# Cross-attention on one core: fewer and larger copies, earlier context loads, less clearing, and one exponential tile in four unsplit

## What is computed

```python
q = (x @ Wq).reshape(B, N, HEADS, hd).transpose(0, 2, 1, 3)
k = (context @ Wk).reshape(B, M, HEADS, hd).transpose(0, 2, 1, 3)
v = (context @ Wv).reshape(B, M, HEADS, hd).transpose(0, 2, 1, 3)
scores = jnp.einsum('bhid,bhjd->bhij', q, k) * scale
scores = jnp.where(context_mask[:, None, None, :], scores, max_neg)
attn = jax.nn.softmax(scores, axis=-1)
out = jnp.einsum('bhij,bhjd->bhid', attn, v)
```

## Time and profile before

| | |
|---|---|
| median of 3 runs | 4101.87 us |
| the profiled execution | 4104.39 us |
| its span | 4102.5 us |
| busy PE, PEld | 3330.3 us (81%), 2553.6 us (62%) |
| busy DVE, ACT, POOL | 2647.3 (65%), 2227.0 (54%), 1061.0 (26%) |
| granted TensorE clock over the span | 0.913 |
| first score product to last value product of the stage | 1752.7 to 2790.6 us |

### The profile page before, as it was taken

One profiled execution on the slowest core, in us unless ns is written; L12 is line 12 of the kernel. 1 busy time (PEld: TensorE's weight loads), 2 busy tenths in 40 slices (PEclk: granted clock), 3 DMA queues, 4 the chain that ended last, 5 costly groups with the idle time before them and its releaser, 6 DMA issues. The chain is left out here.

```text
span 4102.5 us, 50439 instructions
## 1 busy us (share of the span) xinstructions
PE 3330.3 (81%) x15064; PEld 2553.6 (62%) x15064; DVE 2647.3 (65%) x4397; ACT 2227.0 (54%) x4058; POOL 1061.0 (26%) x1139
## 2 busy tenths in 40 slices
PE   5899999999999996377877778775729989950799
PEld 4687877777787875244554455543518877740587
DVE  5787777777777774555655566565653349977554
ACT  4676767667676763155655555563122224448665
POOL 1233333232323232044544444453300000000000
PEclk9999999999999998688988898897969999985899
DMA  4444443444434432333333333324642237779775
GB/s 128 127 131 124 139 123 124 131 134 120 133 120 129 131 108 70 88 96 93 75 88 91 91 80 87 92 61 162 227 141 92 110 118 265 273 279 410 245 247 194
DMA packets 294941, 582.43 MB, mean 142 GB/s; under 512 B 37672, under 2 KB 119600, under 8 KB 280384
## 3 DMA queue, kind: packets, MB, share of 16 engines
q1 hardware_dynamic: 282048, 554.61, 42.6%
q10 hardware_dynamic: 12672, 25.17, 1.7%
HBM read 339.49 MB, written 172.79 MB: 125 GB/s over the span
## 5 line engine op out<-in xcount | busy, mean ns | idle before, releaser
L1555 DVE TENSOR_REDUCE ca_negm<-ca_mx 128x1 fp32r<-128x512 f32 x512 | 353.2, 690 | 433.2 <-PE ca_mx L1701 426.1
L640 POOL TENSOR_SCALAR sa_ex<-sa_ex,sa_rs 128x512 f32<-128x512 f32 x512 | 356.7, 697 | 952.3 <-DVE sa_rs L518 952.3
L513 DVE TENSOR_REDUCE sa_nm<-sa_st 128x1 f32<-128x512 f32 x512 | 351.1, 686 | 269.3 <-PE sa_st L747 268.2
L704 PE MATMUL sa_pj<-sa_xh,sa_w 128*128 128x512 f32 x1536 | 459.7, 419 | 11.7 <-DVE sa_kl L496 9.8
L389 ACT ACTIVATE sa_eh<-sa_tr 128x512 fp32r<-128x512 f32 x512 | 306.7, 599 | 293.9 <-PE sa_tr L757 290.8
L1628 POOL TENSOR_TENSOR ca_el<-ca_ex,ca_eh 128x512 fp32r<-128x512 f32 x256 | 365.5, 1429 | 164.8 <-ACT ca_eh L1484 163.9
L382 ACT ACTIVATE sa_ex<-sa_st,sa_nm 128x512 f32<-128x512 f32 x512 | 351.2, 686 | 58.2 <-DVE sa_nm L513 54.9
L522 DVE TENSOR_TENSOR sa_el<-sa_tr,sa_eh 128x512 fp32r<-128x512 f32 x512 | 351.2, 686 | 36.9 <-ACT sa_eh L389 30.1
L1476 ACT ACTIVATE ca_ex<-ca_st 128x512 f32<-128x512 f32 x512 | 298.2, 589 | 79.2 <-PE ca_st L1719 78.1
L1731 PE MATMUL ca_ov<-ca_eh,ca_vc 128*66 128x512 f32 x512 | 226.7, 443 | 120.0 <-ACT ca_osb L1491 72.2
L757 PE MATMUL sa_tr<-top_ident,sa_ex 128*128 128x128 f32 x2048 | 309.7, 274 | 0.2 <-POOL sa_ex L640 0.2
(11 more groups left out here) (244 smaller groups left out, 7695.9 us busy)
## 6 DMA issues: line engine op xcount, KB each, us to landing
sa_w<-w_split SPq DMA_DIRECT2D x56, 1536.0 KB, 7.4
up_g<-gate SPq DMA_DIRECT2D x50, 512.0 KB, 4.4
gate<-gate_ev SPq DMA_DIRECT2D x24, 1024.0 KB, 3.8
gate<-up_g SPq DMA_DIRECT2D x48, 512.0 KB, 2.9
up<-up_ev SPq DMA_DIRECT2D x24, 1024.0 KB, 5.6
mul_a<-gate SPq DMA_DIRECT2D x48, 512.0 KB, 12.0
mul_b<-up SPq DMA_DIRECT2D x48, 512.0 KB, 13.0
dn_a<-gate SPq DMA_DIRECT2D x96, 256.0 KB, 3.5
```

Of the source, the lines that this page charges most:

```text
L513: nc.vector.tensor_reduce(nm[:, u % U:u % U + 1], st[:, u % 2], AX_X, ALU.max, negate=True).then_inc(dve_mx, 1)
L640: nc.gpsimd.tensor_scalar(ex[:, u % U], ex[:, u % U], rs[:, u % U:u % U + 1], 1.0, ALU.mult, ALU.mult).then_inc(pool_n, 1)
L704: yield nc.tensor.matmul(pj[:, bank], w[:, n % 2, m, part, k], xx[:, b % 2, k], start=(i == 0 and k == 0), stop=(i == 2 and k == DK - 1))
L1555: nc.vector.tensor_reduce(negm[:, n % 2, qt, h:h + 1], mx[:, m % 2], AX_X, ALU.max, negate=True).then_inc(dve_mx, 1)
```

## The change

In the cross-attention stage:

1. The columns of the key and query weights are stored in another order when they are split (`columns`, `split_columns`), so that head j's column d comes to partition 4 d + j of the projections. One DMA from all 128 partitions then fills one part of all four heads (`stack`). A step's stack copies are 3 for keys and 3 for queries, all in slot 8, with one for the mask and, in slot 5, one for the maximum rows. One semaphore for each place of the ring stands for all of them.
2. `cr` has four buffers; all four context tiles of the next batch are loaded in slot 1 of a step with s % 4 = 0. The mask is loaded before x.
3. q4 and k4 are no longer cleared; POOL sets their two rows of ones, and DVE only the ones columns of vc. ACT and DVE no longer wait for this, SP and PE do.
4. Tiles with a % 8 = 3 and 7 are not split: `product` makes one plain float32 matmul of the values and `ex`. ACT then has 4 of 8 high parts, POOL 2; POOL and DVE 3 low parts each. The buffer of `ex` of such a tile is free when its product is made.

```diff
@@ cross_attention_stage
-    HIGH = ("act", "pool", "act", "dve", "act", "pool", "act", "act")
-    LOW = ("pool", "dve", "pool", "dve", "pool", "dve", "pool", "dve")
+    HIGH = ("act", "pool", "act", "", "act", "pool", "act", "")
+    LOW = ("pool", "dve", "pool", "", "pool", "dve", "dve", "")
-        cr = sp.sb("cr", [P, 2, CD])
+        cr = sp.sb("cr", [P, NT, CD])
+        def columns(tile, n):
+
+            if CK <= n < 2 * CK:
+                return tile
+            return tile.rearrange("p (g j d) -> p g d j", j=HS, d=XD)
+
+        def split_columns(tile, n):
+
+            if CK <= n < 2 * CK:
+                return tile
+            return tile.rearrange("p (g d j) -> p g d j", j=HS, d=XD)
@@ sync
+            def stack(n, tile, src, part):
+                e.dma_start(f32(tile[part * XD:(part + 1) * XD, n % RING]), f32(src[:, :])
+                            ).then_inc(stacked[n % RING], 16)
+            def stack_keys(n):
+                r = n % RING
                 if n >= RING:
                     e.wait_ge(pe_st, U * (n - RING) + U)
+                e.dma_start(f32(k4[MR:MR + 1, r]), env["mask_n"][n // XG:n // XG + 1, :].partition_broadcast(HS)).then_inc(stacked[r], 16)
+                e.wait_ge(act_kh, n + 1)
+                stack(n, k4, kh, 0)
+                stack(n, k4, kh, 1)
+                e.wait_ge(pool_kl, n + 1)
+                stack(n, k4, kl, 2)
+            def stack_queries(n):
+                e.wait_ge(act_qh, n + 1)
+                stack(n, q4, qh, 0)
+                stack(n, q4, qh, 2)
+                e.wait_ge(dve_ql, n + 1)
+                stack(n, q4, ql, 1)
             def max_rows(n):
                 e.wait_ge(act_mr, n + 1)
-                for j in range(HS):
-                    e.dma_start(f32(q4[MR + 1:MR + 2, n % RING, j]), f32(mrow[j:j + 1, :])).then_inc(mr_in[n % RING], 16)
+                e.dma_start(f32(q4[MR + 1:MR + 2, n % RING]), f32(mrow[:, :])
+                            ).then_inc(mr_in[n % RING], 16)
...
-                if t == 5 and n < N:
-                    stack_keys(n, range(3), 0)
-                    stack_keys(n, range(3), 1)
-                if t == 7 and n < N:
-                    stack_keys(n, range(3), 2)
                 if t == 8 and n < N:
-                    for part in range(3):
-                        stack_keys(n, range(3, 4), part)
-                    mask_row(n)
-                    for j in range(HS):
-                        stack_queries(n, j)
-                if t == 3 and s >= 0 and s % XG == 1 and s // XG + 1 < B:
-                    load_context(NT * (s // XG + 1))
-                    load_context(NT * (s // XG + 1) + 1)
-                if t in (8, 10) and context_tile(s, t - 1) is not None:
-                    load_context(context_tile(s, t - 1) + 1)
+                    stack_keys(n)
+                    stack_queries(n)
+                if t == 1 and s >= 0 and s % XG == 0 and s // XG + 1 < B:
+                    for i in range(NT):
+                        load_context(NT * (s // XG + 1) + i)
@@ scalar
             def exponent(a):
                 e.wait_ge(pe_st, a + 1)
-                if a >= EX:
+                if a >= EX and LOW[a % 8 - EX]:
                     wait_low(e, a - EX)
+                elif a >= EX:
+                    e.wait_ge(pe_av, a - EX + 1)
...
-                nc.scalar.activation(w_hi[:, n], w_raw[:, n % 2], ACT.Copy).then_inc(act_w, 1)
+                nc.scalar.activation(split_columns(w_hi[:, n], n), columns(w_raw[:, n % 2], n), ACT.Copy).then_inc(act_w, 1)
@@ vector
-            nc.vector.memset(f32(q4[:]), 0.0).then_inc(zeroed, 1)
-            nc.vector.memset(f32(k4[:]), 0.0).then_inc(zeroed, 1)
-            e.wait_ge(zeroed, 2)
-            nc.vector.memset(f32(q4[MR:MR + 2]), 1.0).then_inc(zeroed, 1)
-            nc.vector.memset(f32(k4[MR:MR + 2]), 1.0).then_inc(zeroed, 1)
-            nc.vector.memset(f32(vc[:]), 1.0).then_inc(zeroed, 1)
+            nc.vector.memset(f32(vc[:, :, :, :, 2 * XD:VW]), 1.0).then_inc(ones_set, 1)
@@ gpsimd
+            nc.gpsimd.memset(f32(q4[MR:MR + 2]), 1.0).then_inc(ones_set, 1)
+            nc.gpsimd.memset(f32(k4[MR:MR + 2]), 1.0).then_inc(ones_set, 1)
@@ tensor, product(a)
-                wait_low(e, a)
+                if LOW[a % 8]:
+                    wait_low(e, a)
+                else:
+                    e.wait_ge(act_ex, a + 1)
...
                 values = vc[:, b % 2, kt, HS * g + h]
+                if not LOW[a % 8]:
+                    nc.tensor.matmul(ov[0:VW, :], f32(values), ex[:, a % EX], start=(kt == 0),
+                                     stop=(kt == NT - 1)).then_inc(pe_av, 1)
+                    return
                 nc.tensor.matmul(ov[0:VW, :], values, eh[:, a % EL], start=(kt == 0), stop=False)
                 nc.tensor.matmul(ov[0:VW, :], values, el[:, a % EL], start=False, stop=(kt == NT - 1)).then_inc(pe_av, 1)
```

More of the change, by code:

```diff
@@ L42 @@
 WQMAX = 7.0
-ZEROED = 5
+ONES = 3
 BIG = float(2.0 ** 100)
@@ L1273, in cross_attention_stage @@
         dve_w = sp.sem("dve_w")
-        zeroed = sp.sem("zeroed")
-        cr_in = [sp.sem(f"cr_in{i}") for i in range(2)]
+        ones_set = sp.sem("ones_set")
+        cr_in = [sp.sem(f"cr_in{i}") for i in range(NT)]
         xq_in = sp.sem("xq_in")
@@ L1290, in cross_attention_stage @@
         dve_vl = sp.sem("dve_vl")
-        stacked = [[sp.sem(f"stacked{r}{j}") for j in range(HS)] for r in range(RING)]
-        mask_in = [sp.sem(f"mask_in{r}") for r in range(RING)]
+        stacked = [sp.sem(f"stacked{r}") for r in range(RING)]
         pe_mx = sp.sem("pe_mx")
@@ L1344, in load_context @@
             def load_context(j):
-                if j >= 2:
-                    e.wait_ge(pe_ct, j - 1)
-                e.dma_start(cr[:, j % 2], xs[j]).then_inc(cr_in[j % 2], 16)
+                if j >= NT:
+                    e.wait_ge(pe_ct, j - NT + 1)
+                e.dma_start(cr[:, j % NT], xs[j]).then_inc(cr_in[j % NT], 16)
             def load_x(b):
@@ L1358, in load_mask @@
                 e.dma_start(maskb[:, :], env["mask_f"][b:b + 1, :].partition_broadcast(P)).then_inc(maskb_in, 16)
-            def stack_keys(n, heads, part):
+            def stack(n, tile, src, part):
+                e.dma_start(f32(tile[part * XD:(part + 1) * XD, n % RING]), f32(src[:, :])
+                            ).then_inc(stacked[n % RING], 16)
+            def stack_keys(n):
                 r = n % RING
-                if part == 2:
-                    e.wait_ge(pool_kl, n + 1)
-                else:
-                    e.wait_ge(act_kh, n + 1)
-                for j in heads:
-                    if n >= RING:
-                        e.wait_ge(pe_st, U * (n - RING) + NT * j + NT)
-                    src = kl if part == 2 else kh
-                    e.dma_start(f32(k4[part * XD:(part + 1) * XD, r, j]), f32(src[j * XD:(j + 1) * XD, :])
-                                ).then_inc(stacked[r][j], 16)
@@ L1399, in outputs @@
                             ).then_inc(o_out[j % 2], 16)
-            for i in range(2):
-                load_context(i)
+            load_context(0)
             load_weights(0)
             load_weights(1)
-            for i in range(2, NT):
+            for i in range(1, NT):
                 load_context(i)
@@ L1412, in _ @@
                 load_weights(n)
-            e.wait_ge(zeroed, ZEROED)
+            e.wait_ge(ones_set, ONES)
             for G, s, t in slots():
@@ L1419, in _ @@
                     max_rows(s)
[L1420 to L1435 removed]
+                if t == 8 and n < N:
+                    stack_keys(n)
[3 more added lines that the diff above has]
+                        load_context(NT * (s // XG + 1) + i)
                 if t == 9 and s >= 0 and s % XG == 1 and s // XG + 1 < B:
+                    load_mask(s // XG + 1)
                     load_x(s // XG + 1)
[L1438 removed]
             for i in range(2):
@@ L1451, in high_key @@
                 if n:
-                    for j in range(HS):
-                        e.wait_ge(stacked[(n - 1) % RING][j], 96 * ((n - 1) // RING) + 96)
+                    e.wait_ge(stacked[(n - 1) % RING], STACKS * ((n - 1) // RING) + STACKS)
                 nc.scalar.activation(kh[:, :], km[:, :], ACT.Copy).then_inc(act_kh, 1)
@@ L1659, in transpose_context @@
                 for k in range(CK):
-                    last = nc.tensor.transpose(ms[:, cols(k)], cr[:, j % 2, cols(k)], ident[:, :])
+                    last = nc.tensor.transpose(ms[:, cols(k)], cr[:, j % NT, cols(k)], ident[:, :])
                 last.then_inc(pe_ct, 1)
```

29 lines of the change are left out of this document (8 added, 21 removed).

## The result

The changed kernel takes 3936.22 us (median of 4 runs, 3935.61 to 3937.34); the kernel before took 4103.49 beside it (4 runs, 4101.55 to 4108.8). The ratio is 0.9591, with an interval of 0.9574 to 0.9607: 167 us faster, 101 us above the 3835 forecast and 6 us beyond the upper end of the range. The direction was right, the size was not.

The account below looks back on a forecast made before the run. TensorE was taken as the nearest, not tight, bound, stalled behind SyncE's full queue; 232 us in the stage, 30 at the start and 6 in the first copies, 268 together, gave 3835 us, range 3785 to 3930.

Parts of the forecast that it names:

- The queue: Cross-attention stage, SyncE: 32 issues a step become 8, some 10 us of issuing; the seven copies land before slot 2.
- The context: Cross-attention stage: tiles loaded a step earlier into four buffers remove an 18.6 us stall per kind 1 step, 130.2 us of waits.
- rival B: Queue not relieved or copies late: steps keep near 28 us, only context and start are gained, 3938 us; chance 0.16.
- The start: Kernel start, before the first score product: less clearing and fewer first copies save 36 us, 30 and 6.
- the clearing: Kernel start: five VectorE memsets shrink to one small one, two go to GpSimd; 30 us gained.
- the first copies: First step, before the first maximum product: 19 issues (12 us) shrink to 7 (4.4 us); 6 us gained, between 0 and 8.
- The unsplit tile: Value products, one tile in four unsplit: ScalarE's slot falls to 1.05 us, PE trades two fp32r matmuls for one plain float32.
- P: Price on PE of one plain float32 matmul of 512 columns: taken as 0.94 us, wrong if outside 0.8 to 1.1.
- A: Rival on the value products: plain float32 costs 1.74 us, giving 3920 us; chance 0.10.
- C: Rival on the value products: plain float32 costs 0.44 us, ScalarE bounds, giving 3787 us; chance 0.08.
- bare slots: Slots without projections: 1.2 us forecast from 1.34; staying at 1.34 would mean order of work, not amount, sets their pace.
- Rival D: Slower: the plain product leaves TensorE at its lower clock, stage 1372 us instead of 806; chance 0.03.

Follow-up runs that it names:

- the kernel with four large copies: Changed kernel with the second copies of kh and qh left out from the fourth step on, four of six large copies kept: 3897.66 us.
- the repaired one: Changed kernel with the x load in two separately issued halves and four result buffers: 3880.09 us with unsplit tiles, 3862.15 us with all tiles split.
- x in two parts: Changed kernel with the high half of x issued in slot 7 and the low half in slot 13, each with its own semaphore: 3887.62 us.

## Why the prediction was right or wrong

**The queue: the step that failed.** The prediction had the seven copies "needed in slot 2 of the next step, ten slots or over 12 us later", found 14 us for them one after the other, and then wrote "overlapped they need far less". They do not. From the first issue at 1978.63 to the maximum product at 1993.86 it is 15.2 us, over the one-by-one 14, though the large copies are six and not seven: 1.5 MB, while the mask row has 8 KB. The 14 also priced a copy of 256 KB at the 2.0 us of one of 64 KB. The argument for overlap was the 0.63 us from issue to issue with 2.0 us to landing, at 64 KB each; with four times the bytes at the same spacing it had no row under it. The row to read was the sum of bytes over the time, and the prediction never made it. The cost of this alone is PE's wait for ca_q: about 1.5 us in each of 15 steps, kinds 1 and 2, as the kernel with four large copies shows for kind 1 (25.0 for 26.5).

The same sentence named what is queued behind the copies and went on: "only the x and mask loads and the outputs of slot 12". That *only* is the larger mistake. Nobody waits for the issue of x, but PE waits for its landing, 12.7 to 15.7 us after the issue since it moves only behind the copies, and an output that can't be issued holds ScalarE's buffer. Taking x out, or issuing it elsewhere, gives 53 and 49 us; buffers that no longer wait for the stores give 14, or some 7 once x is cured. Both together, 3936 to 3880, are 56 us of the 93 by which the steps were too long.

**The context: right in kind, wrong in what was late next.** The stall of 18.6 us and the clock after it went, and no wait for ca_cr is left. But "what is late next is TensorE itself" was wrong: the stall had been the time in which x landed. The context alone brings 88 us where 130 stood in the prediction; kind 1 fell by 22 us and kind 2 rose by 10. I took the earlier trace rows as a list of prices, each to be had by removing its wait. Had I asked of every load issued or in flight during the stall when it goes out, when it lands and who needs it, the x loads, issued at 2062.72 with 9.0 us to landing, and ScalarE's slot-by-slot waits behind the same queue, would have been on the path at once. This also means that rival B, which had "the context and the start are gained alone" at 3938, came to the right time by a wrong account. Issuing does not go by bytes (0.6 us for 256 KB), the copies do land late, the steps of kinds 0, 1 and 3 were relieved all the same, and the loss sits in the one kind that B had left untouched.

What the queue change brought is seen by subtraction only: from 4014.75 (context alone) to 3908.89 (context, queue, clearing) are 106 us, 31 of them the clearing, so some 75. In the steps of kinds 0 and 3 it is plain: 26.7 to 23.8 and 29.5 to 26.1, all tiles split.

**The start: right in the clearing, lucky in the sum.** The first projection came at 1673.95 against 1677 forecast, 33.4 us earlier; undoing the clearing costs 31 us where 30 were in the sum. The first score came 33.8 us earlier for 36 forecast, so the first copies, at 6 us in the sum, brought 0.4; the 3.4 us that the clearing brought beyond its 30 hide most of that miss. Two terms within the clearing were off and hidden. The memset on GpSimd takes 5.21 us, not the 9.5 worked out from the ratio of subtractions. And the read with a stride costs. Timelines after, GpSimd and then ScalarE with a strided and a plain split of a weight tile:

```profile
1643.98 5.21 POOL L1619 MEMSET ca_q<- 2x6144 f32 x1 [7.24 <-POOLq L67]
...
1647.18 1.09 ACT L1491 ACTIVATE ca_w_hi<-ca_w_raw 128x512 fp32r<-128x512 f32 x1 [7.80 <-DMA ca_w_raw<-in_L_xattn_Wk_dram]
1653.54 0.63 ACT L1491 ACTIVATE ca_w_hi<-ca_w_raw 128x512 fp32r<-128x512 f32 x1
```

1.09 us for 0.63, and on VectorE 1.04 for 0.69: 0.8 us for each of 7 tiles, some 6 us of engine time, within the 0 to 9 of the prediction. It does not show in the time, as the prediction took it, since loads end the waits there. The Trainium skill (SBUF — State Buffer, Door 1: The DMA port swizzle) says that a read which crosses to a new 16-byte line each time is penalised; the trace agrees that this read, with a stride of 128 bytes, costs more, and these rows are its size here.

**The unsplit tile: the price right, its worth wrong.** A plain float32 product has two records of 590 ns. Group of the value line, and a stretch of PE's timeline around one:

```profile
L1724 PE MATMUL ca_ov<-ca_ex,ca_vc x256: 590/592/1061, 1727.4 to 2621.5; 128*66 128x512 f32 x128
...
1941.75 1.02 PE L1724 MATMUL ca_ov<-ca_ex,ca_vc 128*66 128x512 f32 x2
1942.21 0.80 PE L1708 MATMUL ca_st<-ca_q,ca_k 98*128 98x512 f32 x1
1942.85 0.40 PE L1690 MATMUL ca_mx<-ca_k,ca_q 97*128 97x512 f32 x1
```

From 1941.75 to 1942.85 lie the product and one matmul of 0.234 (the score product, whose row starts before the second pass is through), so P is 0.87 us, two passes of 0.43; 0.94 was forecast, and rivals A (1.74) and C (0.44) fall. The Trainium skill had two answers: the four passes of FP8 and Floating Point Precision (TensorE Precision Notes) agree with 0.87, which is four times 0.22. The factor of four that TensorE: Matmul & The Clock Gate (Terms, the row on the xbus) gives the transpose does not hold against a real product here: 512 columns cost twice the four transposes of 0.109.

What failed is the slot. "The 0.2 above the sum shrinks to 0.15" put bare slots at 1.2 us. Counted from one maximum product to the next they average 1.30 after in kind 0, for 1.35 with all tiles split and 1.34 before: 0.05 gained of 0.14. The prediction had named an outcome close to this, bare slots that stay at 1.34: their pace comes from the order of the work and not from its amount. ScalarE, VectorE and GpSimd had less work and the slot got hardly shorter, while PE's 0.4 us a tile was paid where PE is the bound: the two slots with projections that have an unsplit product last 2.03 us for 1.63. So the unsplit tiles cost 27 us of the changed kernel and 18 of the repaired one. Kinds 0 and 3 missed by 0.7 us each. In kind 0 it is the bare slots: nine of them 0.10 too low are 0.9 us, while its seven slots with projections took (24.2 - 9 x 1.30 - 0.35)/7 = 1.74, close to the 1.76 forecast.

**The clock: right.** Rival D fell. The granted clock of the stage is 0.97, 1.00 in three of the four steps shown, and it falls to between 0.87 and 0.91 after PE's waits in kind 2 alone; with x in two parts five of the seven steps of kind 2 have 1.00 too. The plain product does not lower it: kind 3, with four of them, runs at 1.00.

**What stays open.** The same 86 MB keep the DMA engines busy for 459 us instead of 328. The runs show that it follows the queue change: with all tiles split the share of kinds 0 and 3 is 0.55 and 0.50, for 0.27 and 0.31 before. They don't show whether it is the size of the copies, the six of them starting together, or the 32 partitions that each one writes; copies of 256 KB spaced apart were not tried. Nor is it settled why kind 2 stays longer than kind 3 (29.1 in the repaired kernel with unsplit tiles, 27.7 in kind 3; 29.2 and 26.1 with all tiles split). Of the missing 101 us the stage has 96 (902.2 for 806) and the start 2, and nothing later accounts for much: from the last value product to the end it is 1312.8 us after for 1311.9 before.

## What to carry to other kernels

Before counting a removed wait as gained, list every load issued or in flight during it, with when it goes out, when it lands and who needs it: here the stall on one load had hidden another, and of 22 us gained in one step 10 came back in the next. When issues are merged, count bytes over the time as well as issues, each kind of transfer at a rate read from rows of its own, and ask of each thing queued behind who waits for its landing, not who waits for its issue; a load with a near deadline goes ahead of a burst or well after it. Work moved to the nearest bound is paid at full price, while the engines that it relieves give nothing unless their sum, and not the order of the work, sets the pace.

## What the hardware showed that was not expected

- Six copies of 256 KB from one part of the on-chip memory to another, issued within 5 us, held TensorE, which waits for them, until 15.2 us after the first issue: 1.5 MB at about 103 GB/s. They kept the DMA engines busy throughout at 145 to 150 GB/s of all traffic, where the loads of x ran at 387. Copies of 64 KB had landed in 2.0 us each at a spacing of 0.63.
- For nearly the same bytes (85.54 MB for 86.57) the DMA engines' busy share rose from 31.6% to 51.0%: packets of 2048 bytes were as many as before and took 178 ns each instead of 122.
- An issue on SyncE costs 0.4 to 0.65 us for 2, 192, 256 or 1024 KB alike (the third large copy of a burst 1.56), but behind a burst it stood 6.33 us and 2.79 us, with the engine held all that time.
- A plain float32 product of 512 columns is two passes of 0.43 us, 0.87 together, against 0.234 for one of fp32r.
- A memset of 6144 columns takes GpSimd 5.21 us (2 partitions) and VectorE 5.18 (128), though a subtraction takes GpSimd nearly twice as long (1432 to 780 ns).
